# One transformer stack with two kinds of attention and two mixtures of experts: key sums by TensorE, places by the eight largest, one register load per block, weights loaded behind the attention loop

## The chip, the cores and the metric

One core of a Trainium2 chip runs the whole computation. The core has five engines that run their own instruction streams and meet at semaphores: TensorE (PE, matrix products into PSUM), VectorE (DVE), ScalarE (ACT), GpSimd (POOL) and SyncE (SP, which here only issues DMAs). The metric is the time of one execution on the device in microseconds (us), lower is better.

## The reference

`x` is 1024 tokens of 256 channels. Four residual steps follow each other:

```python
x = x + tanh(g_xattn[0]) * L0_xattn(layernorm(x), ctx)   # 16 heads of 16, fake-quantized q, k, v and softmax
x = x + tanh(g_ffn[0])   * L0_ffn(layernorm(x))          # 32 experts of 176 units, 8 chosen in 4 of 8 groups, + shared 352
x = x + tanh(g_xattn[1]) * L1_xattn(layernorm(x), ctx)   # 8 heads per batch over channels, 32 wide
x = x + tanh(g_ffn[1])   * L1_ffn(layernorm(x))          # 32 experts of 96 units, 6 chosen, + shared 192
```

In `L0_ffn` the sigmoid scores plus a bias are taken in 8 groups of 4; a group's score is the sum of its two largest; four groups stay; the eight largest of what is left are the token's experts, and their scores, normalized, are the weights. `L1_ffn` takes the six largest of 32 directly. In `L1_xattn` a head's output is `softmax(q^T k) v^T`: the softmax divides by the sum of the exponentials over the 256 keys.

## The kernel before

Tokens lie in 8 tiles of 128 (NT = 8). Every engine has its own program, written out as loops over numbered steps; the order in each program is the order of execution, and semaphores join them. After the projections (to about 85 us) come these stages.

**Attention of layer 0.** 128 steps s (tile, head). TensorE computes the scores of 1024 keys (`scores`), VectorE their maximum (`row_max`, L1297), ScalarE the exponential (`exp`, L1156), GpSimd the 8-bit form (`quantize`, L1667), SyncE a transposing DMA (`turn`, L745), TensorE the product with v (`attend`, four steps late). Three times per 32 steps, work for the pair of tiles just finished ("unit" u = 0, 1, 2) is slipped in at fixed places `at` of the window: output projection, norm, router, choice of experts (`choose0`, five parts at 22 to 26), place in each expert's list (`place`, two parts at 27 and 29). `place` turns the 0/1 mask of chosen experts into row numbers: a running count over the experts gives each chosen expert a number 1 to 8 (`kq`), `eq` compares it with 1 to 8, `prod` multiplies with the positions from TensorE's `rank`, and a reduction picks them (L1414, L1425, L1426). With these numbers GpSimd scatters the rows of `xaug` (the normed token, its places and weights) to `xs_dram` by indirect DMA, one instruction per tile and place (`scatter`, L1680): 64 in layer 0, 48 in layer 1. From step 61 on one is sent in every second step.

**Experts' weights.** SyncE loads 44 tiles for gate and up of layer 0 in eleven DMAs of 1 MB, each waiting for the one before it (`tiles_in`, L751): two inside the attention loop at steps 70 and 86, nine behind it. Then come `blocks_in` (register loads from `tab`, then each block's rows, L774, and down weights, L780).

**FFN of layer 0, then of layer 1.** The unit list `units` holds the shared expert (8 tiles in 3 parts, layer 1: 2 parts) and then the routed blocks of 128 rows (95, layer 1: 79). `ffn(layer, i)` is the step of each engine; for TensorE it transposes block q + 1 (L956), does gate and up of q (L993), turns the hidden values of q - 1 (L1005) and does down of q - 2 (L1026). The expert of a block is a number in `tab`, read into registers of TensorE for four blocks at once (`experts_of`, L962). VectorE finds where each row goes, for four blocks at once (`goes_to`, L1501 to L1514), GpSimd scatters the results to `y_dram` (`y_scatter`, L1690). Unit 3 of layer 0 is chosen and placed inside the steps of the shared expert: `choose0` at i = 9, `place` at 12 and 14, `tables` at 14 and 18.

**Sums.** `sums_in` brings the k rows of every token back (`y2`, a ring of 3 in W), and `routed_sum` adds them with a reduction over a strided view (L1545); in layer 0 GpSimd adds the halves of tiles 2 to 7 first (`half_sum`, L1698).

**Attention of layer 1.** 16 steps n: `scores1`, `row_max1` (L1561), `exp1` with the sums of the keys beside it (L1227), `inverse_sum1` (L1569), `normalize1` on GpSimd (L1706), `turn1`, `turned1`, and per tile `attend1` (L1080) and `tile_out1` (L1582). The sums of layer 0 are worked in at steps 1, 5 and 9, and the choice and places of layer 1 at step 13 and later; unit 3 is done inside the steps of layer 1's shared expert.

## Time and profile before

| | us |
|---|---|
| median of 3 runs | 984.89 (984.3 to 984.92) |
| the profiled execution | 984.9 |
| its span | 983.2 |

| stage | us from the span's start |
|---|---|
| projections and preparation | 0 to 85 |
| attention of layer 0 | 85 to 317 |
| shared expert, places of unit 3, weights | 317 to 388 |
| 95 routed blocks of layer 0 | 388 to 627 |
| sums and attention of layer 1 | 627 to 750 |
| shared expert, scatters of layer 1 | 736 to 804.5 |
| 79 routed blocks of layer 1 | 812 to 948 |
| sums of layer 1, output | 948 to 983 |

Busy over the span: TensorE 730.5 us, VectorE 584.4, GpSimd 500.0, ScalarE 444.1. How to read it: no engine is busy all the time, and each stage has its own bound. So a change is priced stage by stage: which engine or which transfer ends the waits there.

### The profile page before, as it was taken

What the parts mean: (1) busy time and instruction counts of PE and PEld (TensorE: products, weight loads), DVE (VectorE), ACT (ScalarE), POOL (GpSimd) and SP (SyncE); (2) the same over time, 40 slices, a digit from 0 to 9 for tenths busy, and PEclk for the clock granted to TensorE, in tenths of its full rate; (3) what the DMA queues carried; (4) which work ended last, traced back from release to release, by engine and by line L of the source; (5) the groups of instructions that cost most, each with busy time, mean ns of one, the idle gap of its engine ahead of it and who ended that gap; (6) DMA issues with size and microseconds to landing.
All of it is one profiled execution on the core that took longest, in us unless ns stands there. A gap on an engine that the chain in (4) does not pass through costs nothing.

```text
span 983.2 us, 19955 instructions
## 1 busy us (share of the span) xinstructions
PE 730.5 (74%) x5595; PEld 540.4 (55%) x5595; DVE 584.4 (59%) x1344; ACT 444.1 (45%) x1057; POOL 500.0 (51%) x579
## 2 busy tenths in 40 slices
PE   5638777677776875999999999435587649998940
PEld 4625445445454663777777777323355537777730
DVE  5997878968878372444444444275665615454538
ACT  4536787566674211444444444224462105555630
POOL 4433676588887632333333333235558754555530
PEclk9867778576585897999999999756776879999985
DMA  8905999799998875666666666682006435555546
GB/s 278 340 1 105 182 171 158 131 218 205 194 185 172 255 245 168 199 193 205 189 203 184 203 186 188 223 345 106 1 2 191 165 121 162 187 161 186 172 159 203
DMA packets 221971, 175.49 MB, mean 178 GB/s; under 512 B 146586, under 2 KB 200810, under 8 KB 220842
## 3 DMA queue, kind: packets, MB, share of 16 engines
q1 hardware_dynamic: 207866, 132.52, 53.3%
q0 software_dynamic: 13728, 41.17, 11.6%
q8 instruction: 50, 0.82, 0.4%
q14 instruction: 55, 0.45, 0.1%
q10 hardware_dynamic: 272, 0.52, 0.1%
HBM read 87.92 MB, written 52.69 MB: 143 GB/s over the span
## 4 chain that ended last, share of the span: by engine, by line
POOL 26%; issue 24%; PE 15%; DVE 11%; DMA 9%; ACT 5%; SPq 0%; POOLq 0%; DVEq 0%; ACTq 0%
POOL y_dram L1690 12%; POOL xs_dram L1680 6%; DMA pT<-p 6%; ACT e L1156 5%; DVE acc L1545 4%; POOL p L1667 4%; PE psum L993 4%; PE psum L1026 3%; DVE nmax L1297 2%; POOL W L1706 2%; PE psum L982 1%; PE psum L956 1%; PE psum L860 1%; POOL W L1698 1%; DMA W<-y_dram 1%
## 5 line engine op out<-in xcount | busy, mean ns | idle before, releaser
L1690 POOL DMA_INDIRECT y_dram<-ybuf,idxi x174 | 166.9, 959 | 232.2 <-ACT ybuf L1205 225.3
L1493 DVE COPY hT<-psum 88x256 f32<-88x256 f32 (+2 forms) x214 | 74.3, 347 | 241.4 <-PE psum L1005 241.2
L993 PE MATMUL psum<-W,xTs 128*128 x696 | 195.6, 404 | 10.9 <-issue 6.5
L1156 ACT ACTIVATE e<-psum,nmax 128x1024 f32<-128x1024 f32 x128 | 142.5, 1113 | 75.8 <-POOL p L1667 44.2
L1297 DVE TENSOR_REDUCE nmax<-psum 128x1 f32<-128x1024 f32 x128 | 153.0, 1220 | 35.9 <-PE psum L860 23.6
L1667 POOL TENSOR_SCALAR p<-e 128x1024 f16<-128x1024 f32 x128 | 134.5, 1051 | 74.8 <-ACT e L1156 50.3
L860 PE MATMUL psum<-kstack,qstack 128*128 128x512 bf16 x256 | 108.9, 521 | 46.7 <-ACT e L1156 43.0
L1680 POOL DMA_INDIRECT xs_dram<-xaug,posi x112 | 110.1, 983 | 49.2 <-issue 33.2
L993 PEld LDWEIGHTS psum<-W,xTs 128*128 128x128 f32 x696 | 115.0, 191 | 36.0 <-issue 16.0
L1195 ACT ACTIVATE sg<-psum 128x176 f32<-128x176 f32 (+2 forms) x214 | 60.9, 285 | 149.1 <-PE psum L993 83.5
L1205 ACT ACTIVATE ybuf<-psum,dot 128x256 f32<-128x256 f32 x174 | 82.4, 474 | 101.0 <-PE psum L1026 100.6
L873 PEld LDWEIGHTS psum<-osb_v,pT 128*128 128x128 f16 x1024 | 68.0, 104 | 47.9 <-DMA pT<-p 27.3
L956 PE MATMUL psum<-ident,xs 128*128 128x128 f32 x348 | 67.8, 276 | 25.4 <-DMA xs<-xs_dram 25.4
L873 PE MATMUL psum<-osb_v,pT 128*128 128x16 f16 x1024 | 72.0, 176 | 16.5 <-DMA pT<-p 16.0
L1186 ACT ACTIVATE xTs<-psum 128x256 f32<-128x256 f32 x174 | 65.4, 376 | 31.8 <-PE psum L956 31.8
L1005 PE MATMUL psum<-ident,h 128*88 128x128 f32 (+2 forms) x309 | 71.0, 280 | 10.1 <-DVE h L1485 9.6
L956 PEld LDWEIGHTS psum<-ident,xs 128*128 128x128 f32 x348 | 49.7, 143 | 44.0 <-DMA xs<-xs_dram 26.2
L874 PEld LDWEIGHTS psum<-osb_v,unlift 128*128 128x128 f16 x1024 | 62.8, 104 | 19.6 <-issue 16.0
L874 PE MATMUL psum<-osb_v,unlift 128*128 128x16 f16 x1024 | 68.5, 172 | 0.0
L1482 DVE TENSOR_TENSOR h<-sg,psum 128x176 f32<-128x176 f32 (+1 forms) x174 | 66.5, 382 | 0.0
L1005 PEld LDWEIGHTS psum<-ident,h 128*88 128x88 f32 (+2 forms) x309 | 39.5, 128 | 44.5 <-issue 16.5
L1545 DVE TENSOR_REDUCE acc<-W 128x256 f32<-128x1536 f32 (+2 forms) x16 | 40.6, 2537 | 23.0 <-DMA W<-y_dram 23.0
(238 smaller groups left out, 1221.5 us busy)
## 6 DMA issues: line engine op xcount, KB each, us to landing
xs<-xs_dram SPq DMA_DIRECT2D x174, 160.0 KB, 3.2
W<-in_wffn SPq DMA_DIRECT2D x17, 1024.0 KB, 6.9
xs_dram<-zeros SPq DMA_DIRECT2D x2, 5120.0 KB, 25.5
oT<-in_wffn SPq DMA_DIRECT2D x96, 88.0 KB
osb_v<-in_wffn SPq DMA_DIRECT2D x94, 88.0 KB
W<-y_dram SPq DMA_DIRECT2D x8, 1024.0 KB, 6.5
W<-y_dram SPq DMA_DIRECT2D x8, 768.0 KB, 4.5
W<-in_wffn SPq DMA_DIRECT2D x4, 768.0 KB
```

The source lines that it names most:

```text
L860: last = pe.matmul(bank(s_bank(s) + n), qstack[:, t // TH, head, t % TH * P:(t % TH + 1) * P], kstack[:, head, n * BANK:(n + 1) * BANK], s ...
L873: pe.matmul(out, pT[:, s % PT_RING, k, :], v, start=k == 0, stop=False)
L874: last = pe.matmul(out, unlift[:, :], v, start=False, stop=k == NT - 1)
L956: last = pe.transpose(ps[:, k * P:(k + 1) * P], xs[:, slot, k * P:(k + 1) * P], ident[:, :])
L993: last = pe.matmul(out, xTs[:, n % 2, k, :], Wv[layer][:, k, :, :, bass.DynSlice(of_block[q], 1), :], start=k == 0, stop=k == KD - 1)
L1005: last = pe.transpose(bank(4)[0:rows, c * P:(c + 1) * P], h[:, q % 2, c * rows:(c + 1) * rows], ident[:, :])
L1156: act.activation(e[:, s % 2, :], bank(s_bank(s), 2), ACT.Exp, bias=nmax[:, s % S_RING:s % S_RING + 1], accum_out=esum[:, t, head:head + 1] ...
L1205: act.activation(ybuf[:, b % Y_RING, :], bank(5 + item(q) % 2)[:, 0:D], ACT.Copy, scale=dot[:, b % XS_RING, 1:2]).then_inc(cf["y_sb"], 1)
L1297: dve.tensor_reduce(nmax[:, s % S_RING:s % S_RING + 1], bank(s_bank(s), 2), AX.X, ALU.max, negate=True).then_inc(c2["max"], 1)
L1667: pool.tensor_scalar(p16[:, s % P_RING, :], e[:, s % 2, :], PMAX, LIFT, ALU.mult, ALU.add).then_inc(c2["p16"], 1)
L1680: pool.indirect_dma_start(xs_dram[layer][:, :], bass.IndirectOffsetOnAxis(posi[:, t, k:k + 1], 0), xaug[:, t, :], None).then_inc(scattered ...
L1690: pool.indirect_dma_start(y_dram[layer][:, :], bass.IndirectOffsetOnAxis(idxi[:, slot:slot + 1], 0), ybuf[:, b % Y_RING, :], None).then_in ...
```

## The change

Nine edits in one step:

1. `place` drops `kq`, `eq` and `prod`. The positions are multiplied with the mask, and `max` (the eight largest of each token) gives the row numbers, whose base is one higher. It now has four parts, `choose0` six; in a window they stand at 17 to 24 and 27, 28. The group search of `choose0` takes six sums of pairs and one maximum.
2. The other work of a window moves to earlier steps (projection 9 to 7, router 17 to 13, and so on). In the tail `place` and `tables` move from i = 12, 14, 14, 18 to 9, 10, 11, 12, 16.
3. No weight is loaded inside the attention loop: eleven DMAs stand behind it.
4. TensorE loads one expert per block, `expert_in(q + 1)`, behind `gate_up(q)`.
5. `goes_to` is cut in three parts, done one group of four blocks ahead.
6. `normalize1`, `inverse_sum1` and the key sums of `exp1` go. `attend1` adds eight products with a matrix of ones, which give the key sums of every output element; `tile_out1` divides by them.
7. Sums are made of `tensor_tensor` additions in place; GpSimd makes more of them in layer 0 and the first of every second tile in layer 1. The ring `y2` has 4 places, the last of them in `xs`.
8. SyncE loads `y2` of layer 0 first, the weights of layer 1 and its shared expert behind that.
9. The choice and the places of layer 1 for all four units lie in the attention loop of layer 1, and GpSimd sends no scatter of layer 1 between its other work.

```diff
-XS_RING, Y_RING, Y2_RING, IDX = 8, 4, 3, 4
+XS_RING, Y_RING, Y2_RING, IDX = 8, 4, 4, 4
...
-                    if s in (70, 86):
-                        sp.wait_ge(c2["scores"], STEPS // 2)
-                        tiles_in(0, 16 + (s - 70) // 4, 4, cw["gu0"])
-                        loaded += 1
                 sp.wait_ge(c2["scores"], STEPS)
-                for first in (0, 4, 8, 12, 24, 28, 32, 36, 40):
+                for loaded, first in enumerate((16, 20, 0, 4, 8, 12, 24, 28, 32, 36, 40)):
...
-                    sp.wait_ge(cw["gu0"], 16 * loaded)
+                    if loaded:
+                        sp.wait_ge(cw["gu0"], 16 * loaded)
                     tiles_in(0, first, 4, cw["gu0"])
...
+                def expert_in(q):
+                    layer, _, b, _ = units[q]
+                    if b == 0:
+                        pe.wait_ge(cp["tab"], layer + 1)
+                    _, of_block[q] = nc.values_load_multi_w_load_instructions(
+                        tab[0:1, 1, b:b + 1], engines=(mybir.EngineType.PE,), min_val=0, max_val=EXPERTS - 1)
...
                     if q < end:
                         gate_up(q)
+                    if q + 1 < end and routed(q + 1):
+                        expert_in(q + 1)
...
+                    for k in range(2):
+                        for j in range(PER_TILE):
+                            last = pe.matmul(bank(0)[j * HD1:(j + 1) * HD1, D:2 * D], ones[:, 0:HD1],
                                              a1pT[t % 2][:, j, k, :], start=k == 0, stop=k == 1, skip_group_check=True)
...
-                        step(dve.tensor_tensor(prod_, eq_, over_places(pos[:, :, :]), ALU.mult))
-                        step(dve.tensor_reduce(posf[:, :, 0:k], prod_, AX.X, ALU.add))
-                        dve.tensor_copy(posi[:, here, 0:k], posf[:, :, 0:k]).then_inc(cp["placed"], 1)
+                        step(dve.tensor_tensor(pos[:, :, :], pos[:, :, :], mask[:, here, :], ALU.mult))
+                    else:
+                        pick_first(pos, posf, 2)
+                        dve.tensor_scalar(posi[:, here, 0:k], posf[:, :, 0:k], 1.0, None, ALU.subtract).then_inc(cp["placed"], 1)
...
+                        if b % IDX and b - b % IDX + IDX < BLOCKS[layer]:
+                            goes_to(layer, b - b % IDX + IDX, b % IDX - 1)
...
-                    step(dve.tensor_reduce(acc[:, t % 2, :], y2[:, t % Y2_RING, 0:k * D].rearrange("p (k d) -> p d k", k=k),
-                                           AX.X, ALU.add))
+                        step(dve.tensor_tensor(y[:, 0:n], y[:, 0:n], y[:, n:2 * n], ALU.add))
+                    if layer == 1:
+                        step(dve.tensor_tensor(y[:, D:2 * D], y[:, D:2 * D], y[:, 2 * D:3 * D], ALU.add))
+                    elif not pooled(layer, t):
+                        step(dve.tensor_tensor(y[:, 0:2 * D], y[:, 0:2 * D], y[:, 2 * D:4 * D], ALU.add))
+                    step(dve.tensor_tensor(acc[:, t % 2, :], y[:, 0:D], y[:, D:2 * D], ALU.add))
...
-                    dve.scalar_tensor_tensor(x[:, t, :], bank(0)[:, 0:D], tgate[:, 1:2], x[:, t, :], ALU.mult,
-                                             ALU.add).then_inc(cx["x"], 1)
+                    step(dve.reciprocal(inv1[:, :], bank(0)[:, D:2 * D]))
+                    dve.scalar_tensor_tensor(inv1[:, :], bank(0)[:, 0:D], tgate[:, 1:2], inv1[:, :], ALU.mult,
+                                             ALU.mult).then_inc(cx["out"], 1)
+                    dve.wait_ge(cx["out"], t + 1)
+                    dve.tensor_tensor(x[:, t, :], x[:, t, :], inv1[:, :], ALU.add).then_inc(cx["x"], 1)
...
-                half_sum(2)
-                half_sum(3)
...
+                half_sum(0, 2)
+                half_sum(0, 3)
+                for u in range(1, NT // 2):
+                    if u == NT // 2 - 1:
+                        norm_rstd(pool, step, 0, 0, cn[2]["stats"], cn[2]["rstd"])
+                    norm_rstd(pool, step, 2 * u, u, cn[1]["stats"], cn[1]["rstd"], 1.0 / SCALE1 ** 2)
+                    if u < NT // 2 - 1:
+                        half_sum(0, 2 * u + 2)
+                        half_sum(0, 2 * u + 3)
+                norm_rstd(pool, step, 2, 1, cn[2]["stats"], cn[2]["rstd"])
+                for i in range(NT * TOP[1]):
+                    scatter(1, i)
+                    if i == 5:
+                        norm_rstd(pool, step, 4, 2, cn[2]["stats"], cn[2]["rstd"])
+                    elif i == 15:
+                        norm_rstd(pool, step, 6, 3, cn[2]["stats"], cn[2]["rstd"])
```

## Rows read from the trace of the kernel before

**Rows 1.** Windows: busy us (instructions) of PE, PEld, DVE, ACT, POOL; clock; DMA share, GB/s.

```profile
285.40:316.40 31.00, 22.60 (x324) 14.49 (x321) 28.12 (x59) 18.21 (x33) 24.04 (x23) 0.61 0.96 178
316.40:388.00 71.60, 47.21 (x273) 38.66 (x273) 28.06 (x129) 12.14 (x35) 33.42 (x37) 0.81 0.75 229
388.00:627.00 239.00, 238.54 (x1143) 176.11 (x1141) 110.56 (x312) 101.11 (x284) 89.67 (x94) 1.00 0.61 187
652.30:732.60 80.30, 48.03 (x322) 32.59 (x321) 52.42 (x105) 40.05 (x145) 43.46 (x81) 0.71 0.19 70
812.40:943.80 131.40, 120.12 (x702) 100.84 (x702) 64.96 (x255) 76.68 (x231) 71.56 (x75) 1.00 0.53 168
```

**Rows 2.** Waits of SyncE's queue, 320 to 380 us: total us, times, longest us.

```profile
SPq L751 <- DMA W<-in_wffn: 40.3, 7, 7.8
SPq L787 <- DMA xs_dram<-xaug,posi: 8.8, 1, 8.8
```

**Rows 3.** Chain of waits, 376 to 392 us: start, us, what.

```profile
378.98 0.03 SPq L787
...
382.17 2.21 DMA xs<-xs_dram
...
388.31 2.14 PE psum L993 x4
```

**Rows 4.** The same view at the last scatters of layer 1.

```profile
800.79 0.96 POOL xs_dram L1680
...
802.05 2.50 DMA xs_dram<-xaug,posi
```

**Rows 5.** Timeline of TensorE at two neighbouring blocks of layer 1: start, us.

```profile
854.14 0.81 PE L993 MATMUL psum<-W,xTs 128*128 x4
...
855.56 0.81 PE L993 MATMUL psum<-W,xTs 128*128 x4
```

**Rows 6.** Groups by shape, whole span: busy us, mean ns, idle before.

```profile
L1545 DVE TENSOR_REDUCE acc<-W 128x256 f32<-128x1536 f32 x8 | 21.9, 2731 | 9.5 <-DMA W<-y_dram 9.5
...
L1698 POOL TENSOR_TENSOR W<-W 128x1024 f32<-128x1024 f32 x6 | 13.9, 2342 | 0.0
...
L1545 DVE TENSOR_REDUCE acc<-W 128x256 f32<-128x2048 f32 x2 | 7.2, 3587 | 13.4 <-DMA W<-y_dram 13.4
...
L466 DVE TENSOR_TENSOR tok<-tok,inv 128x2048 f32<-128x2048 f32 x2 | 4.6, 2291 | 0.1
...
L463 DVE RECIPROCAL inv<-step_of 128x128 f32<-128x128 f32 x2 | 1.9, 952 | 0.1
```

**Rows 7.** The same of VectorE, 338 to 357 us (tail).

```profile
L1425 DVE TENSOR_TENSOR prod<-eq,pos 128x512 f32<-128x512 f32 x1 | 0.7, 693 | 0.0
```

**Rows 8.** Timeline of VectorE in the attention loop: start, us.

```profile
311.64 1.52 DVE L1425 TENSOR_TENSOR prod<-eq,pos 128x512 f32<-128x512 f32 x1
```

**Rows 9.** Windows of 32 exponentials each (L1156 alone): ACT busy, clock, DMA.

```profile
192.10:254.98 62.88, 37.82 (x64) 0.66 1.08 210
254.99:317.66 62.67, 37.82 (x64) 0.64 0.99 182
```

**Rows 10.** Chain of waits behind the last block of layer 0.

```profile
627.73 5.90 DMA y_dram<-ybuf,idxi
```

**Rows 11.** VectorE by shape in layer 1's attention, 652.3 to 732.6 us.

```profile
L1545 DVE TENSOR_REDUCE acc<-W 128x256 f32<-128x1024 f32 x6 | 11.6, 1928 | 0.0
...
L1547 DVE TENSOR_TENSOR x<-x,acc 128x256 f32<-128x256 f32 x6 | 2.5, 424 | 0.2
...
L1569 DVE RECIPROCAL a1rs<-a1sum 128x4 f32<-128x4 f32 x14 | 2.4, 169 | 1.1 <-ACT W L1227 1.1
```

**Rows 12.** TensorE's queue at a register load, 850.8 to 852.4 us: ns, first and last start.

```profile
L962 PEldq FUSED_REGOPS  x4: 146/148/151, 851.3 to 852.1; - x4
...
L962 PEldq TENSOR_LOAD <-tab x1: 330/330/330, 850.9 to 850.9; - x1
```

**Rows 13.** The same queue's wait ahead of gate_up, 852.3 to 853.4 us.

```profile
L991 PEldq EVENT_SEMAPHORE  x2: 51/51/51, 852.4 to 853.3; - x2
```

More of the change, by code:

```diff
@@ L140, in build @@
         mout = sb("mout", [P, 2, EXPERTS + 2])
-        pairs = [sb(f"pairs{i}", [P, 2, GROUPS]) for i in range(8)]
+        pairs = sb("pairs", [P, 2, GROUPS, 6])
         gpad = sb("gpad", [P, 2, GROUPS + 8 - GTOP])
@@ L150, in build @@
         kx = sb("kx", [P, 2, EXPERTS])
-        kq = sb("kq", [P, 2, EXPERTS])
         pos = sb("pos", [P, 2, EXPERTS])
@@ L830, in _ @@
                     sums_in(0, t)
-                    if 2 <= t < 6:
-                        tiles_in(1, 4 * t, 4, cw["gu1"])
+                shared_in(1)
+                for first in range(0, TILES[1], 4):
+                    tiles_in(1, first, 4, cw["gu1"])
                 sp.wait_ge(cx["pT_ps"], 2 * PAIRS1)
@@ L1264, in _ @@
                 norm_apply(act, 0, 0, cn[1]["rstd"], cn[1]["xn"])
-                for i in range(2 * NT + 6):
+                for i in range(2 * NT + 8):
+                    u, at = divmod(i - 9, 4)
+                    if at == 0 and 0 <= u < NT // 2:
+                        norm_apply(act, 2 * u, u, cn[2]["rstd"], cn[2]["xn"])
+                    elif at == 1 and 0 <= u < NT // 2:
+                        x_out(1, u)
+                    elif at == 2 and 0 <= u < NT // 2:
+                        route_out(1, u)
                     if i < 2 * NT and i % 4 == 3 and i // 4 < 3:
@@ L1350, in choose0 @@
[L1350 to L1357 removed]
+                        four = sf.rearrange("p t (g i) -> p (t g) i", g=GROUPS)
@@ new lines, in goes_to @@
+                    if part == 0:
+                        step(dve.tensor_tensor(own[:, 0:n, :], expert_no[:, :].unsqueeze(1).to_broadcast([P, n, EXPERTS]),
+                                               block_expert[:, blocks].unsqueeze(2).to_broadcast([P, n, EXPERTS]),
+                                               ALU.is_equal))
+                    elif part == 1:
+                        for i in range(b, b + n):
+                            dve.wait_ge(xs_in[i % XS_RING], 16 * ring_turn(layer, i, XS_RING))
+                        step(dve.tensor_tensor(both[:, 0:n, :, :], xs[:, slots, D:].rearrange("p n (c e) -> p n c e", c=2),
+                                               own[:, 0:n, :].unsqueeze(2).to_broadcast([P, n, 2, EXPERTS]), ALU.mult))
+                    else:
+                        if ring_turn(layer, b, XS_RING) > 1:
+                            dve.wait_ge(cf["y_sb"], done_before(layer, b + n - 1, XS_RING))
+                        step(dve.tensor_reduce(dot[:, slots, :], both[:, 0:n, :, :], AX.X, ALU.add))
+                        step(dve.copy_predicated(idxf[:, blocks], filled[:, blocks], dot[:, slots, 0]))
+                        for i in range(b, b + n):
+                            earlier = ring_turn(layer, i, Y_RING) - 2
+                            if earlier > 0:
+                                dve.wait_ge(y_out[i % Y_RING], 16 * earlier)
+                        dve.tensor_copy(idxi[:, slots], idxf[:, blocks]).then_inc(cf["idx"], n)
@@ L1610, in _ @@
                     elif i == 9:
-                        for part in range(5):
+                        for part in range(6):
                             choose0(part, 3)
+                        place(0, 0, 3)
+                    elif i == 10:
+                        place(1, 0, 3)
+                    elif i == 11:
+                        place(2, 0, 3)
+                        place(3, 0, 3)
                     elif i == 12:
-                        place(0, 0, 3)
-                    elif i == 14:
-                        place(1, 0, 3)
@@ L1718, in _ @@
                         sent += 1
-                while sent < 44:
+                while sent < 42:
                     scatter(0, sent)
```

343 lines of the change are left out of this document (121 added, 222 removed).

## The prediction

> **What bounds the kernel now.** I read the windows first, stage by stage, then the chain of waits inside each, then the groups by shape for the prices. Six stretches matter. In the attention loop of layer 0 the 15 steps that hold the choice and the places take 31.0 us, and VectorE is busy for 28.1 of them [rows 1]: these steps are VectorE's, 2.07 us each, while elsewhere GpSimd and the transposing DMAs set a shorter step. In the tail (316 to 388) no engine is full; its end is a chain of transfers [rows 2, 3]. The 95 blocks of layer 0 are TensorE's alone: 238.5 busy of 239.0 [rows 1]. The attention of layer 1 runs at 80.3 us with VectorE at 52.4 and TensorE at 48.0 at a clock of 0.71, so it lives on waits between engines. From 736 to 804.5 GpSimd issues scatters, one every 1.26 us [rows 4], 48 of them: 60.5 us. The 79 blocks of layer 1 take 131.4 us for 78 distances, 1.685 each [rows 1], though two neighbours without a register load stand 1.42 apart [rows 5]. Behind them come eight sums of 2.73 us [rows 6].
>
> **Attention loop, three windows: -10 us.** Per unit VectorE loses `eq` and `prod` (0.69 each without company) and the reduction (of the same size), `kq` and four small operations (some 0.6 together), and gets two eight-largest, a product and a subtraction (0.5): 2.2 us less (0.69 from [rows 7]). Beside GpSimd `prod` took 1.52 instead of 0.69 [rows 7, 8]: 0.8 us of waiting goes with it. So 3 us per window, three windows, 9. The new parts are below 1 us each, so a step is 1.22 for the maximum plus at most 1; the two long steps go, and nothing new comes late but GpSimd, whose two quantizations and one scatter fill about 3.5 us of two steps. The two loads that leave the loop cost little: the 32 exponentials beside them took 62.9 us, the next 32 took 62.7 [rows 9]. I take 1. Bounds: 3 x 2.2 = 6.6 less 1.6 for worse places of the other work, and 3 x 4 + 2 = 14. I take 10, nearest to the rows.
>
> The Trainium skill (SBUF — State Buffer, section "SBUF: two separate sides") says that a VectorE operation with two SBUF inputs and a GpSimd operation that reads SBUF exclude each other for the whole instruction. The 1.52 against 0.69 agrees. That rule speaks against edit 7, and it is weighed there.
>
> **Tail: +4 us.** The chain of loads begins when the last transpose is issued (320.4). Seven of its waits sum to 40.3, 5.8 each, with 0.4 for the issue [rows 2]. The wait for the scatters ended 8.8 us after the last load was issued, at 378.98 [rows 2, 3], so that load was issued at 370.2 and would land at about 376.5. Two more in the chain: the eleventh is issued near 382.1. SyncE then takes 3.2 us for its registers (378.98 to 382.17), so the first block's rows are asked for at about 385.9 instead of 382.2, behind half a load, and land at 388.5 instead of 384.4; 3.9 us on, the first routed gate_up (388.3 before [rows 3]) begins at 392.2, all relative to the end of the loop: +4. The places of unit 3 come about 4 us earlier (i = 11 for 14, and 2.2 us less work), the scatters are done by about 375, and that is covered: the weights are late now. Bounds: 0 (loads at 5.2 without scatters beside them, rows asked for in their shadow) to +7.
>
> **Blocks of layer 0: 0 us.** TensorE is full; a register load every block runs in its queue while matmuls of 2.49 us drain. If that cover failed, it would cost up to 0.68 x 95 = 65 us; the third rival.
>
> **End of layer 0 to the last scatter of layer 1: -28 us.** (a) The last result row landed after 5.90 us because weights went ahead of it (edit 8); the unloaded value nearest is the 2.50 of a scatter [rows 4, 10]: -3.5. (b) Sums of tiles 0 and 1: 3.59 + 0.42 each now [rows 6, 11]; as additions 128x1024 (half of 2.29, with overhead 1.2), 128x512 (0.69), twice 0.42 and gaps, 2.9: -2.3 for both. So the first maximum of the attention comes at 652.3 - 5.8 = 646.5. (c) From there to the first placement (732.6 before) VectorE was busy 52.4. Edits: six reductions of 1.93 become one addition of 0.42 each, -9.0; the small reciprocals go, -2.4 [rows 11]; choice and place, -1.9; placement one step earlier in the program, two maxima and a copy less, -3.1; and five `tile_out1` gain a reciprocal of 128x256. A reciprocal of 128x128 took 0.952 [rows 6], so 1.8, with 0.4 for one more addition: +2.2 each, +11. That leaves 47. GpSimd's normalizing is gone, but each half sum grows from 2.34 [rows 6] to some 3.5, and VectorE's additions wait for it; TensorE gets as many more matmuls per tile as `attend1` has now. Of the 28 us of waits (80.3 - 52.4) I keep 16: the start (norm, scores), two or three collisions with half sums, and slow-clock matmuls. First placement: 646.5 + 63 = 710. (d) GpSimd has nothing else left then, so 48 scatters run through: 48 x 1.26 = 60.5, two norms of 1.4, landing 2.5: 776 instead of 804.5. Placements of the other units come every 13 to 15 us or faster, ahead of 12 scatters (15.2); the 16 steps of the shared expert begin behind the last placement (about 745) and end before 776 too. Bounds: no waits at all, 696 and -42; all 28 kept, 721 and -17. I take -28.
>
> **Blocks of layer 1: -10 us.** One load of four registers takes TensorE's queue 1.5 us (850.9 to 852.4 [rows 12, 13]; 0.33 for the load, then 0.29 per register), and TensorE stood still for part of it [rows 12]. One register per block is then 0.39 + 0.29 = 0.68. Between two passages of the same wait the queue needed 0.9 us (0.86) for a whole block without a load [rows 13]. 0.86 + 0.68 = 1.54, above TensorE's 1.42 [rows 5]: the queue becomes the bound, at 1.54 per block. 78 x (1.685 - 1.54) = 11.3; some stalls at the block ring stay, 10. The three parts of `goes_to` take away what delayed `down` once in four blocks, inside the same 1.54. Bounds: fully hidden, 1.42 and -20; each load fully open, 1.42 + 0.68 = 2.10 and +32.
>
> The rule that speaks against this edit is in the Trainium skill (DMA: Bandwidth & Descriptors, "Latency and other measured facts"): a register load has a floor of about 600 ns, and the compiler takes four at once to amortize it. The row has 0.33 for the instruction, less than that floor; what the floor would make of the time is rival 5.
>
> **Last sums: -3 us.** A tile costs VectorE 2.73 + 0.42. An even tile becomes 0.95 + three of 0.42, 2.4 with gaps; an odd one 1.76 on GpSimd (3/4 of 2.34 [rows 6]) and 1.35 on VectorE. If the two engines exclude each other, as `prod` shows, a pair costs 2.4 + 1.76 + 1.35 = 5.5 against 6.2: 2.8 for four pairs. If they overlap, 8.
>
> **Sum.** -10 + 4 - 28 - 10 - 3 = -47. The profiled execution took 984.9 (1.7 around its span of 983.2), the median of the runs is 984.89: 938.
>
> **The rivals.** (1) The register loads hide wholly: 1.42 per block, 928. For: in layer 0 the same load costs nothing; against: 0.86 + 0.68 > 1.42. (2) VectorE keeps all its waits in the attention of layer 1, now for half sums and for TensorE's products: -17 in place of -28, 949. For: the reciprocal and the longer half sums stand on the same two engines; against: the normalization that held TensorE is gone. (3) Slower than before: the queue has no room, and every register load is open, 0.68 us in each of 95 blocks (+65) and 2.10 per block in layer 1 (+32 in place of -10): 984.9 - 10 + 4 - 28 - 3 + 97 = 1045. It decides the sign as soon as 0.33 us of every load are open in both layers: 95 x 0.33 = 31 and 78 x (0.33 - 0.265) = 5 are 36, against the 37 gained in the other stages. For: each load of four cost layer 1 up to 1.06 us (4 x (1.685 - 1.42)). Against: 238.5 of 239.0 in layer 0 with 1.5 us loads in it. (4) The loop gains only 4 and the weights cost 7: the loads take what the loop gave, 947. (5) A load that stands alone holds the queue longer than the load in front of a group of four: in a group the three further registers lie in the shadow of the first answer, so the 0.33 of the row is only the part that shows. The whole group is 1.5; if a quarter of the 0.87 of those three was such shadow, a single load holds 0.68 + 0.21 = 0.89, the queue needs 0.86 + 0.89 = 1.75 per block, above 1.685, and layer 1 loses 78 x 0.065 = 5: 984.9 - 10 + 4 - 28 + 5 - 3 = 953. For: no row shows a load alone. Against: each of the four register instructions has a length of its own behind the load, 0.15 [rows 12]. The floor of 600 ns named above would be this case.
>
> **How the numbers follow.** Forecast 0.5, rival 1 0.15, rival 2 0.17, rival 4 0.08, rival 5 0.05, rival 3 0.05. The range 915 to 962 holds the forecast with its bounds (-14 to -5, 0 to +7, -36 to -17, -20 to -3, -8 to 0, not all at once), rivals 1, 2, 4 and 5; outside are rival 3 and the far ends. What this kernel can tell from no change is 0.2%, 2 us. Faster 0.94, same 0.01, slower 0.05.
>
> **What would show it.** Steps 17 to 28 of a window at most 2.2 us apart, and no 1.5 us `prod`. The eleventh load landing after the last scatter of unit 3. Layer 0's blocks still 2.49 apart with TensorE above 99%. The first scatter of layer 1 near 710 less the earlier gain of 6, then 48 in a row. Blocks of layer 1 1.54 apart with even gaps; 1.42 means rival 1. Reciprocals of 1.8 us in `tile_out1`. Wrong would be: blocks of layer 0 longer than 2.49, or scatters waiting for placements of later units.

## The result

The changed kernel takes 951.29 us (median of 4 runs, 948.25 to 955.92) against 984.9 of the kernel before (4 runs, 984.3 to 985.09): a ratio of 0.9664, with an interval of 0.962 to 0.9708. Forecast was 938 with a range of 915 to 962. The profiled execution took 949.4 us with a span of 947.6, so the span is 35.6 shorter; 47 were forecast.

The table cuts both spans at the same instructions: first and last exponential of layer 0, first gate_up, last scatter of results, first maximum of layer 1, first and last scatter of `xaug`, first and last gate_up. The last column is the forecast term. All come from one profile each; how far the changed kernel's profiles differ stands ahead of the experiments.

| stretch | before | after | difference | forecast |
|---|---|---|---|---|
| to the first exponential | 86.5 | 84.9 | -1.6 | 0 |
| attention loop of layer 0 | 229.9 | 220.5 | -9.4 | -10 |
| tail, to the first gate_up | 71.7 | 75.0 | +3.3 | +4 |
| blocks of layer 0, to the last scatter | 239.6 | 243.7 | +4.1 | 0 |
| to the first maximum of layer 1 | 24.6 | 18.7 | -5.9 | -5.8 |
| to the first scatter of layer 1 | 83.5 | 65.0 | -18.5 | -22 for these |
| first to last scatter of layer 1 | 66.2 | 69.9 | +3.7 | two rows |
| to the first gate_up of layer 1 | 10.3 | 10.4 | +0.1 | 0 |
| 78 distances of blocks of layer 1 | 131.4 | 121.8 | -9.6 | -10 |
| to the end | 39.4 | 37.7 | -1.7 | -3 |

Six rows came within 1.3 us of their term, and the 1.6 us of the start are its own spread (84.6 to 86.7 over the profiles of the changed kernel and its variants). Two terms failed: the blocks of layer 0 (+4.1 for 0) and the scatters of layer 1 (the two rows give -14.8 for -22). These two are 11.3 us; the span lies 11.4 above the sum, and what is left cancels.

### The profile page after: what moved, and what is told of

Its sections match the earlier page's. It is cut to its first block, busy times and chain, and to the rows that moved or that the text cites. A ratio compares the mean times of both kernels' runs of the same rounds, so it can differ in the third digit from the quotient of the medians.

```text
span 947.6 us, 20145 instructions
## 1 busy us (share of the span) xinstructions
PE 741.3 (78%) x5723; PEld 545.1 (58%) x5723; DVE 552.8 (58%) x1322; ACT 438.9 (46%) x993; POOL 485.8 (51%) x524
## 4 chain that ended last, share of the span: by engine, by line
PE 37%; DMA 16%; POOL 13%; DVE 9%; issue 8%; ACT 5%; SPq 2%; POOLq 0%; DVEq 0%; ACTq 0%
PE psum L974 13%; PE psum L1007 10%; DMA W<-in_wffn 6%; DMA pT<-p 6%; POOL y_dram L1652 5%; ACT e L1134 4%; POOL xs_dram L1642 4%; POOL p L1629 4%; PE psum L941 3%; PE psum L986 2%; DVE nmax L1268 2%; DMA W<-y_dram 2%; PE psum L845 2%; DVE a1nb L1528 1%; DVE inv L1542 1%
## 5 line engine op out<-in xcount | busy, mean ns | idle before, releaser
L1134 ACT ACTIVATE e<-psum,nmax 128x1024 f32<-128x1024 f32 x128 | 142.5, 1114 | 60.8 <-POOL p L1629 41.8
L1629 POOL TENSOR_SCALAR p<-e 128x1024 f16<-128x1024 f32 x128 | 133.8, 1045 | 66.4 <-ACT e L1134 42.6
L1164 ACT ACTIVATE xTs<-psum 128x256 f32<-128x256 f32 x174 | 65.4, 376 | 34.8 <-PE psum L941 34.8
L941 PEld LDWEIGHTS psum<-ident,xs 128*128 128x128 f32 x348 | 50.0, 144 | 46.8 <-DMA xs<-xs_dram 28.8
L986 PE MATMUL psum<-ident,h 128*88 128x128 f32 (+2 forms) x309 | 69.9, 277 | 7.2 <-DVE h L1439 4.1
L986 PEld LDWEIGHTS psum<-ident,h 128*88 128x88 f32 (+2 forms) x309 | 39.2, 127 | 39.4 <-issue 16.4
L1007 PE MATMUL psum<-W,hT 96*128 x158 | 54.4, 427 | 0.0
```

The costliest lines, as they stand in the source:

```text
L941: last = pe.transpose(ps[:, k * P:(k + 1) * P], xs[:, slot, k * P:(k + 1) * P], ident[:, :])
L986: last = pe.transpose(bank(4)[0:rows, c * P:(c + 1) * P], h[:, q % 2, c * rows:(c + 1) * rows], ident[:, :])
L1007: last = pe.matmul(out, hT[0:rows, q % 2, c * P:(c + 1) * P], w, start=part == 0 and c == 0, stop=ends(q) and c == parts - 1)
L1134: act.activation(e[:, s % 2, :], bank(s_bank(s), 2), ACT.Exp, bias=nmax[:, s % S_RING:s % S_RING + 1], accum_out=esum[:, t, head:head + 1] ...
L1629: pool.tensor_scalar(p16[:, s % P_RING, :], e[:, s % 2, :], PMAX, LIFT, ALU.mult, ALU.add).then_inc(c2["p16"], 1)
```

## The profile after

Windows of the changed kernel, columns as in [rows 1]: end of the attention loop, tail, blocks of layer 0, attention of layer 1 to the first placement, blocks of layer 1.

```profile
284.90:305.40 20.50, 15.65 (x222) 10.10 (x220) 18.51 (x38) 13.07 (x22) 16.82 (x17) 0.58 1.06 180
305.40:380.40 75.00, 48.21 (x289) 39.70 (x290) 25.94 (x122) 12.18 (x36) 34.32 (x38) 0.77 0.84 253
380.40:624.10 243.70, 239.70 (x1143) 176.68 (x1141) 102.11 (x312) 101.20 (x284) 90.87 (x94) 0.99 0.59 182
642.90:706.90 64.00, 51.34 (x386) 33.75 (x385) 54.24 (x95) 33.14 (x80) 25.36 (x31) 0.77 0.40 146
788.20:909.90 121.70, 121.65 (x701) 101.12 (x701) 59.97 (x258) 76.70 (x231) 71.53 (x75) 0.99 0.57 180
```

Against [rows 1], layer 0 holds the same 1143 matmuls in 243.7 us with 239.7 busy: 4 us of standing still, where there was 0.5. TensorE's timeline shows that it is one place, between the gate_ups of blocks 4 and 5. The lines are blocks 3, 4 and 5, counted from 0:

```profile
387.19 1.35 PE L974 MATMUL psum<-W,xTs 128*128 x4
389.68 1.35 PE L974 MATMUL psum<-W,xTs 128*128 x4
395.91 2.38 PE L974 MATMUL psum<-W,xTs 128*128 x4
```

6.23 us in place of 2.49. The chain of waits there names the cause (start, us, what), and the waits of VectorE from 380 to 396 us its size:

```profile
388.82 3.68 DMA xs<-xs_dram
...
392.62 0.44 DVE both L1460
...
393.43 0.45 DVE h L1436
```

```profile
DVE both L1460 <- DMA xs<-xs_dram: 5.5, 1, 5.5
```

L1460 is the second part of `goes_to`, now one group ahead: at block 2 VectorE waits for the rows of blocks 4 to 7, the last of which SyncE asked for at 388.8, and the hidden values (`h`) that TensorE needs stand behind that wait in VectorE's queue.

The scatters of layer 1 do not run through. GpSimd's timeline at its two norms (in brackets the idle time ahead):

```profile
714.35 0.96 POOL L1642 DMA_INDIRECT xs_dram<-xaug,posi  x1 [0.30 <-issue]
720.30 0.23 POOL L268 TENSOR_SCALAR shift<-mv 128x2 f32<-128x2 f32 x1 [4.99 <-DVE mv L262]
...
733.70 0.96 POOL L1642 DMA_INDIRECT xs_dram<-xaug,posi  x1 [0.30 <-issue]
736.62 0.23 POOL L268 TENSOR_SCALAR shift<-mv 128x2 f32<-128x2 f32 x1 [1.96 <-DVE mv L262]
```

The norms of units 2 and 3 stand after scatter 6 and 16, and GpSimd waits 4.99 and 1.96 us for VectorE's statistics with the places of more scatters in hand.

VectorE by shape from 642.9 to 706.9 us (answers to [rows 11]):

```profile
L1542 DVE RECIPROCAL inv<-psum 128x256 f32<-128x256 f32 x5 | 8.7, 1748 | 0.0
L1515 DVE TENSOR_TENSOR acc<-W 128x256 f32<-128x256 f32 x4 | 4.1, 1026 | 0.0
```

The reciprocal costs 1.75 us, close to the 1.8 taken from the 128x128 one. The additions of `acc` have 1.03 on average for 0.42 without company. Four additions of this window, each beside a half sum of GpSimd's, took 1.07 to 2.24 us; together with the other 13 of their shape they are 5.2 us over 0.42 each.

TensorE's queue at one register load in layer 1 (answers to [rows 12]):

```profile
L949 PEldq TENSOR_LOAD <-tab x2: 300/301/302, 850.7 to 852.2; - x2
L949 PEldq FUSED_REGOPS  x1: 151/151/151, 851.1 to 851.1; - x1
L949 PEldq SEQ_ASSERT  x1: 18/18/18, 851.3 to 851.3; - x1
```

One load per 1.5 us, no longer than one in front of a group of four (0.33).

At the end (timeline of VectorE and GpSimd, then the last instructions of GpSimd's and VectorE's queues), an addition of 0.42 takes 1.91 beside GpSimd:

```profile
927.26 2.23 POOL L1662 TENSOR_TENSOR xs<-xs 128x768 f32<-128x768 f32 x1 [1.74 <-DMA xs<-y_dram]
927.88 1.91 DVE L1512 TENSOR_TENSOR W<-W 128x256 f32<-128x256 f32 x1
929.82 0.43 DVE L1515 TENSOR_TENSOR acc<-W 128x256 f32<-128x256 f32 x1
```

```profile
L732 POOLq DRAIN  x1: 8443/8443/8443, 938.9 to 938.9; - x1
L732 DVEq DRAIN  x1: 464/464/464, 941.9 to 941.9; - x1
```

## The experiments

Each was timed in rounds with the kernel before. Times are medians, the ratio is to the kernel before, and stretches are those of the table, from one profile each. Where a stretch is unedited, the profiles differ: the loop has 220.5 to 223.1 us, the tail 74.3 to 79.7 (eight profiles), the blocks of layer 0 241.6 to 245.6 where they have the stall, the 78 distances of layer 1 121.3 to 125.4 (nine), first to last scatter 68.0 to 70.0. The end, 37.3 to 38.2, is steady, and so is the usual distance of two blocks of layer 1, 1.53 to 1.54 at the median. A smaller difference than these spreads shows nothing.

The times need the same care. Ten runs of the changed kernel lie between 948.3 and 957.4 us. Only e8 and e10 lie wholly below them; the medians of e4, e5 and e9 are below the lowest, that of e1 above the highest. For e2, e3, e6 and e7 the time alone shows nothing, and the reading is that of the stretches.

**The changed kernel again (e0).**

> The changed kernel once more, nothing edited, to learn its own spread: its four times lay between 948.3 and 955.9 us, those of the kernel before within 0.8 us. If the spread belongs to the kernel, five more rounds fall in the same 8 us band around 951 and a second profile shows which stage carries it. I expect the variable part in one of two places: the stall at the fourth and fifth block of layer 0 (3.9 us in the first profile), or the eleven weight loads behind the attention loop (65.6 us for eleven). If the spread came from one odd process only, all fall within 1 us of each other.

952.98 us, six runs from 948.4 to 957.4. The spread belongs to the kernel; in these rounds the kernel before spread too (981.8 to 987.7). The stall at blocks 4 and 5 is in every profile with this order, of 2 to 6 us, mostly 4. What varies most over the profiles is the tail, by the weight loads (eleven took 64.9 us where the tail has 74.3, and 69.9 where it has 79.7): the second of the two places named. The blocks of layer 1 vary too, by a wait of the third part of `goes_to`, where VectorE waits for result scatters to land. Its total, number and longest, 788 to 910 us:

```profile
DVE idxi L1471 <- DMA y_dram<-ybuf,idxi: 9.9, 17, 1.4
```

In e5 one scatter took longer (chain of waits), and two neighbouring distances were 3.42 and 2.73:

```profile
847.66 5.64 DMA y_dram<-ybuf,idxi
```

**Loads of four again (e1).**

```diff
-                    _, of_block[q] = nc.values_load_multi_w_load_instructions(
-                        tab[0:1, 1, b:b + 1], ...
+                    if b % IDX == 0:
+                        _, four = nc.values_load_multi_w_load_instructions(tab[0:1, 1, b:b + n], ...
+                        for i, one in enumerate(four):
+                            of_block[q + i] = [one]
```

> Only the number of registers per load is undone: four experts at once in every fourth block, at the same place behind gate_up. Theory (TensorE's queue): the load of four holds the queue 1.55 us, more than the work that lies in front of TensorE covers, so the pattern of 1.42, 1.6, 2.1, 1.5 per four blocks comes back in layer 1, 1.66 on average for 1.54 to 1.56 now: +8 us (+6 to +11), all in the 79 blocks of layer 1; layer 0 stays at 2.49. Rival (the gain came from goes_to in three parts, which no longer delays down): layer 1 stays at 1.54 to 1.56 and the time within 1 us.

960.1 us (0.9746, 0.9715 to 0.9776). The 78 distances took 132.6 us for 121.8: +10.9, at the theory's upper end (+7 against the longest of the nine profiles, and the time is 7 to 9 above the changed kernel's medians). The gate_ups of three blocks:

```profile
850.91 0.82 PE L978 MATMUL psum<-W,xTs 128*128 x4
853.33 0.81 PE L978 MATMUL psum<-W,xTs 128*128 x4
854.75 0.81 PE L978 MATMUL psum<-W,xTs 128*128 x4
```

2.42, then 1.42 three times: about 1.0 of a load's 1.55 us is open and 0.56 hidden, which is 1.42 - 0.86. With one register 0.68 - 0.56 = 0.12 is open: 1.54. The rival fell.

**One register per block in the kernel before (e11),** the same edit from the other side.

```diff
-                    if kind == "routed" and index % IDX == 0:
-                        ...
-                        for i, expert in enumerate(experts_of(layer, index)):
-                            of_block[q + i] = expert
...
                     if q < end:
                         gate_up(q)
+                    if q + 1 < end and routed(q + 1):
+                        expert_in(q + 1)
```

> The kernel before with edit 4 alone: one expert register per block, read behind gate_up of the block before; goes_to stays whole, in every fourth block. Theory (the load is hidden in layer 0 and the queue is the bound in layer 1): no stall at blocks 4 and 5 of layer 0 (that belonged to goes_to one group ahead), 239.6 us from first gate_up to last scatter as before, and in layer 1 1.54 to 1.6 for three of four blocks with a longer fourth where goes_to delays down: 78 distances in 122 to 127 us for 131.4, -5 to -9, about 977 for 985. Rival (goes_to in three parts is half of the gain): 127 to 131 us, -1 to -4. If the stall belonged to the register loads, layer 0 gets 4 us longer.

974.31 us (0.989, 0.9859 to 0.9921). The windows for the blocks of both layers:

```profile
387.90:626.90 239.00, 237.88 (x1143) 175.41 (x1141) 109.78 (x312) 101.15 (x284) 90.08 (x94) 1.00 0.61 188
810.60:932.00 121.40, 121.28 (x702) 100.69 (x701) 65.30 (x257) 76.69 (x231) 71.49 (x75) 1.00 0.57 181
```

121.4 for 131.4: the edit gives 10 us alone (11 in the time), more than expected, and `goes_to` in three parts gives nothing measurable to layer 1. Layer 0 has no stall at blocks 4 and 5, so that one belongs to edit 5.

**No bounds check in TensorE's queue (e9).**

```diff
-                        tab[0:1, 1, b:b + 1], engines=(mybir.EngineType.PE,), min_val=0, max_val=EXPERTS - 1)
+                        tab[0:1, 1, b:b + 1], engines=(mybir.EngineType.PE,), min_val=0, max_val=EXPERTS - 1,
+                        skip_runtime_bounds_check_because="tab's experts are held to 0 to 31 by tables")
```

> The instruction that checks the loaded expert's bounds is left out of TensorE's queue (the values are held to 0 to 31 where tab is written). Theory (in layer 1 the queue is the bound at 1.51 to 1.54 us per block): the instruction stands 0.14 us of it (851.24 to 851.38), so the distance falls to 1.42 to 1.45 and layer 1's 78 distances give back 5 to 8 us; layer 0, TensorE-bound at 2.49, gives nothing. Rival (VectorE and ScalarE, not the queue, set 1.54): no change in layer 1.

947.14 us (0.9618, 0.9594 to 0.9642); 78 distances in 117.5 us for 121.7. In the queue the register operation of 0.15 us went with the check, so that the load alone is left:

```profile
L949 PEldq TENSOR_LOAD <-tab x1: 303/303/303, 849.8 to 849.8; - x1
```

Most distances are now 1.42, TensorE's own (65 of 78 are at most 1.44; 2 with the check); single ones of 1.6 to 3.6 us remain, one load among the 77 took 0.70. So the queue was the bound at 1.54, as the forecast had it. The gain, 4.2, is below the 5 to 8 expected: 0.11 per block would be 8.6, but the waits for result scatters have 14.5 us here for 9.9. As they vary from profile to profile (e8 has 13.2 with the check), the 4.2 says less than the 0.11.

**The second group at block 4 (e2).**

```diff
+                        if b == IDX:
+                            for part in range(3):
+                                goes_to(layer, IDX, part)
-                        if b % IDX and b - b % IDX + IDX < BLOCKS[layer]:
+                        if b > IDX and b % IDX and b - b % IDX + IDX < BLOCKS[layer]:
```

> goes_to for the second group of four blocks is done whole at block 4, not in parts at blocks 1 to 3; all other groups as in the change. Theory: in layer 0 VectorE stood at block 2 in its wait for the rows of block 7, which SyncE had asked for last (landed 392.5 us), with the product of the hidden values queued behind it; distances of 6.23 and 3.52 for 2.49. With the group later the stall goes: -4 us in layer 0's first ten blocks, and at most -1 at the first distance of layer 1 (2.56). Rival: the rows of blocks 4 and 5 are themselves late because SyncE issues 1.55 us of DMAs per block and reads its tables twice: then TensorE waits there instead and 0 to -1 is seen.

949.99 us (0.9649, 0.9616 to 0.9682), and 243.2 us for the blocks of layer 0: nothing gained. Neither theory held as put. The distances of blocks 4 to 6 are 2.49, but those at 7 and 8 are 3.07 and 5.73: the stall moved one group on. What stops VectorE is not the place of one group but that SyncE is not far enough ahead for any of them.

**SyncE's tables early (e5).**

```diff
                     tiles_in(0, first, 4, cw["gu0"])
+                    if loaded in (8, 9):
+                        sp.wait_ge(cp["tab"], 1)
+                        early[IDX * (loaded - 8)] = table_of(0, IDX * (loaded - 8))
```

> SyncE reads the rows and experts of the first eight blocks while the ninth and tenth weight loads are under way (tab was ready at 352), not behind the last one. No DMA is moved but by that. Theory (SyncE's lead sets the stall at blocks 4 and 5, since goes_to one group ahead asks for rows two blocks earlier than before, and SyncE needs 4 x 1.56 + 3.2 = 9.4 us per four blocks against 9.96 of TensorE, so it cannot catch up): SyncE is 3.2 us earlier at block 0 and 6.4 at block 4. First gate_up about 3 us earlier (377.5), of the stall of 3.9 us some 0.7 is left: -5 to -6. Rival (rows land late because the DMA engines are still full of weights): the stall stays at 3 to 4 us and the start moves by 0 to 1.

946.35 us (0.9618, 0.9596 to 0.9641). The stall is gone, all distances from the third on are 2.49, and the blocks take 239.8 us for 243.7. So SyncE's lead was it (e10, with the tables early too, has no stall either): edit 5 asks for rows two blocks sooner, and a SyncE that needs 9.4 us per four blocks of 9.96 cannot make up for that but by a stall. The start did not move (tail 75.2): xs asked for at 372.3 landed 5.8 us later, behind the last weights, and the last 1 MB landed at 377.5.

**Two loads in the loop again (e4).**

```diff
                     turn(s)
+                    if s in (70, 86):
+                        sp.wait_ge(c2["scores"], STEPS // 2)
+                        tiles_in(0, 16 + (s - 70) // 4, 4, cw["gu0"])
```

> Edit 3 alone is undone: two of the eleven weight loads lie at steps 70 and 86 of the attention loop again, nine behind it. Theory (the weights end the tail): in the changed kernel the last load landed at 376.1 us, the last scatter of unit 3 twelve us earlier (issued 360.4, about 363 landed). With nine loads the last lands 5.9 x 2 = 12 us earlier, level with the scatters; the loop gets 1 us longer: first block at about 370 for 380.5, -9 to -11 in all, near 941. Rival (in the loop the DMA engines are full, share 0.96 to 1.08, so 2 MB more delay the transposes by as much as they save behind it): loop 6 to 10 us longer, total within 3 us of the changed kernel.

947.26 us (0.963, 0.9603 to 0.9657). The tail took 68.3 us for 74.3 to 79.7, the loop 224.4 for 220.5 to 223.1. The exponentials of the window that holds both loads, first of the changed kernel, then of this one:

```profile
187.87:247.15 59.28, 37.59 (x64) 0.59 1.03 189
```

```profile
188.26:251.46 63.20, 37.82 (x64) 0.62 1.08 210
```

+3.9 us for two loads where I had put 1 (the same window, 56.9 us from first to last exponential in the changed kernel, has 56.9 to 57.9 in all profiles without loads and 60.8 here: 3 to 4), and -7 behind the loop where 12 were expected (6 to 11 below the eight tails): between theory and rival. The comparison in [rows 9] had misled. Without loads the second window is 1.4 us shorter than the third (56.9 and 58.3, first to last exponential), so two equal windows did not mean free loads; how much VectorE's long steps hid there stays open.

**Two loads in flight (e8).**

```diff
-                    if loaded:
-                        sp.wait_ge(cw["gu0"], 16 * loaded)
-                    tiles_in(0, first, 4, cw["gu0"])
+                    done = cw[("gu0", "gu0b")[loaded % 2]]
+                    if loaded > 1:
+                        sp.wait_ge(done, 16 * (loaded // 2))
+                    tiles_in(0, first, 4, done)
```

> The eleven weight loads behind the attention loop alternate between two semaphores, so that two are under way and not one; nothing else. Theory (the chain is serial and leaves the DMA engines idle between a landing and the next transfer: DMA share 0.84 in the tail, 5.1 us for the shortest, 6.0 on average): eleven take 50 us or less for 65.6, the last lands by 363, and the scatters of unit 3 (issued to 360.4, landed 363) become the end: first routed gate_up 370 to 373 for 380.5, and -4 to -10 for the time, as the stall at blocks 4 and 5 stays. Rival (the DMA engines are full, the scatters pay for the loads): last landing 1 to 3 us earlier, scatters later, total 0 to -2.

945.27 us (0.9585, 0.9565 to 0.9605), five runs within 3.4 us. Eleven loads took 48.6 us (313.3 to 361.9) for 64.9 to 69.9, and the tail 66.8 for 74.3 to 79.7. What the DMA queues moved in 40 slices of the stretch of the loads, in the changed kernel and in this one:

```profile
GB/s 226 211 331 348 341 135 284 388 86 112 394 316 56 357 405 199 191 391 54 101 336 407 208 227 390 421 159 325 314 351 188 247 386 35 241 358 11 202 400 210
```

```profile
GB/s 221 217 207 250 207 356 280 402 427 402 407 407 413 338 388 375 378 333 244 347 295 347 362 414 277 211 350 309 299 362 399 173 287 255 320 384 415 423 393 288
```

With one load at a time the rate falls to 11 to 112 GB/s between loads. The theory held: the chain was serial, not full. (The first gate_up is at 375.2 and not at 370 to 373, since this loop ended 2.9 us later.)

**Norms later (e3).**

```diff
-                    if i == 5:
+                    if i == 11:
                         norm_rstd(pool, step, 4, 2, cn[2]["stats"], cn[2]["rstd"])
-                    elif i == 15:
+                    elif i == 23:
```

> GpSimd makes the norms of units 2 and 3 of layer 1 after scatter 12 and 24, not after 6 and 16. Theory A: the two waits of GpSimd inside the scatters (4.99 and 1.96 us) are a plain loss from the in-order queue; without them the scatters end 7 us earlier, about 944 for a profile of 949.4. Theory B: behind them stands the placement of unit 1, which came at 728.4; 12 scatters from 707.9 end at 723.1, so the same queue then waits 5 us for it, and only the second norm's wait is gained: -2.5 us (-1 to -3.5).

949.48 us (0.9656, 0.9626 to 0.9687). First to last scatter 66.2 us for 69.9, -3.7. GpSimd's next idle time:

```profile
730.30 1.07 POOL L1642 DMA_INDIRECT xs_dram<-xaug,posi  x1 [3.22 <-DVE posi L1381]
```

Behind the order in GpSimd's queue stands the placement of unit 1: theory B. But not all of the 3.7 is the edit. This profile ran at a higher granted clock of TensorE's, and so did that of e5, whose order of norms is the old one. From 30 us behind the first maximum to the first scatter, in the changed kernel, here and in e5:

```profile
672.90:707.90 35.00, 28.82 (x230) 19.52 (x229) 30.96 (x64) 18.50 (x45) 9.09 (x16) 0.81 0.02 7
```

```profile
678.80:710.50 31.70, 25.71 (x232) 16.92 (x229) 30.41 (x64) 18.02 (x44) 8.59 (x16) 0.94 0.01 3
```

```profile
670.30:702.00 31.70, 25.68 (x232) 16.88 (x229) 30.40 (x64) 18.05 (x44) 8.61 (x15) 0.94 0.02 6
```

The two with 0.94 have the first scatter 61.7 us after the first maximum, the others, at 0.81 to 0.87 and without an edit ahead of it, 64.4 to 65.4. That the clock is the cause is likely but not shown (TensorE was busy for 25.7 us in place of 28.8). e5 has 68.0 from first to last scatter, so against it the norms gain 1.8; against the changed kernel, e10 (clock 0.86, the same norms later) gains 2.7. So the order is 1.8 to 2.7 of the 7 us lost.

**Transposes behind the products (e7),** on top of e3: `x_transposed(1, u)` behind `attend1` on TensorE, `x_out` behind `turned1` on ScalarE.

```diff
-                    if at == 0 and 0 <= u < NT // 2:
-                        x_transposed(1, u)
...
                         attend1((i - 4) // 2)
                     if at == 0 and 0 <= u < NT // 2:
+                        x_transposed(1, u)
                         route(1, u)
```

> On top of the norms after scatter 12 and 24: in layer 1's attention the transposes of the normed tokens (x_transposed) stand behind attend1 of the same step in TensorE's order, and ScalarE's copy of them behind its exponentials; before, TensorE waited 1.9 and 3.4 us for ranked with the turns of the attention behind it. Theory (TensorE's order holds the placement of unit 1, which came at 728.4 and for which GpSimd then waits 4.5 us): the placement comes 2 to 4 us earlier and so does the last scatter: 63 to 64 us from first to last scatter for 66.2. Rival (the chain of unit 1 is bound by its own length: transposes, router, choice, rank, places, 20 us): no gain, or a loss of up to 2 because the copy of unit 0 now comes later.

952.2 us (0.9656, 0.9627 to 0.9685). First to last scatter 65.1, 1.1 less than in e3, but the first scatter came 66.4 us after the first maximum (61.7 in e3, 65.0 in the changed kernel). Between last result and last scatter it is 3.4 us slower than e3: the rival. But e3 had the high clock, and this profile has 0.81. Against e10, whose norms stand in the same place at 0.86, it is 0.8 us slower (150.1 for 149.3). How much of this is the edit stays open; a gain is not shown.

**Last sums on VectorE alone (e6).**

```diff
-                    return t >= 2 if layer == 0 else t % 2 == 1
+                    return layer == 0 and t >= 2
-                for t in range(1, NT, 2):
-                    half_sum(1, t)
```

> GpSimd's share in the last sums is left out: all eight tiles are added by VectorE (0.95 + three of 0.42, 2.34 us a tile with gaps). In the changed kernel VectorE's additions of 0.42 us took 1.9 beside GpSimd, and the sums lasted 20.8 us (921.5 to 942.3) plus the output. Theory (the two engines exclude each other, so the share of GpSimd buys nothing): 8 x 2.34 = 18.7, -2 us (-1 to -4, the last also for the tile that waited 1.8 us for GpSimd behind its own load). Rival (GpSimd takes a real part): +2, eight tiles at 2.34 are behind the loads and the overlap is lost.

948.86 us (0.9624, 0.9597 to 0.9652). From the last gate_up to the end 32.3 us for 37.7: -5.4, more than either bound. The sums give 2.7 (18.1 us for 20.8). The other 2.7 lies behind them: GpSimd's drain takes 8.4 to 8.8 us, behind an addition and behind scatters (8.76 in the kernel before, where it is hidden). In the changed kernel it ran from 938.9 to 947.4, 2.9 us past the output's landing at 944.4; here it starts behind the scatters and is hidden:

```profile
L732 POOLq DRAIN  x1: 8660/8660/8660, 918.3 to 918.3; - x1
```

**All together (e10):** two loads in flight, SyncE's first two tables read before its wait for the scatters (both layers), no bounds check, norms later, last sums on VectorE. The edit that no other experiment has:

```diff
+                    early = {b: table_of(layer, b) for b in (0, IDX)}
                     sp.wait_ge(scattered[layer], 16 * NT * TOP[layer])
                     for b in range(BLOCKS[layer]):
                         if b % IDX == 0:
-                            table = table_of(layer, b)
+                            table = early[b] if b in early else table_of(layer, b)
```

> Two loads in flight, the tables of the first eight blocks read before the wait for the scatters (both layers), no bounds check, norms after scatters 12 and 24, the last sums on VectorE alone. From the changed kernel's 951: tail -8, stall at blocks 4 and 5 -4, attention and scatters of layer 1 -3.5, tables of layer 1 -1.5, blocks of layer 1 -6, last sums -2: -25, 926. If the parts collide (the rows of the first blocks behind the last weights, a scatter queue that is not the end any more), 935.

918.61 us (0.9324, 0.9288 to 0.936): 33 us below the changed kernel, 7 more than expected. Tail, blocks of layer 0, blocks of layer 1 and end:

```profile
307.80:371.00 63.20, 48.95 (x290) 40.32 (x291) 25.84 (x122) 12.15 (x35) 34.26 (x38) 0.82 0.91 297
371.00:610.20 239.20, 237.96 (x1142) 175.76 (x1141) 102.40 (x312) 101.14 (x284) 90.26 (x95) 1.00 0.60 186
...
766.40:884.40 118.00, 113.90 (x703) 99.77 (x702) 60.15 (x259) 76.70 (x231) 71.45 (x75) 1.00 0.59 187
884.40:916.60 32.20, 2.82 (x13) 1.61 (x11) 18.29 (x37) 2.14 (x5) 4.30 (x5) 0.60 0.67 249
```

Against the changed kernel's profile: tail -11.8, layer 0 -4.5, attention and scatters of layer 1 -4.3, scatters to first gate_up 6.9 for 10.4 (the tables), blocks of layer 1 -3.8, end -5.4, and +2.4 before the tail.

## Why the prediction was right, and where it was not

**Attention loop.** The sum was right (-9.4 for -10; -6.8 to -9.4 over the unedited profiles), its parts were not. Windows 1 and 3, from first to last exponential, lost 3.9 and 3.1 us; window 2, which held both loads, lost 4.7, and with the loads put back (e4) only 0.8 (61.6, 56.9 and 60.8 us). So the loads cost 3 to 4 where I took 1, and VectorE's part is about 8 where I took 9. One sign was missed: steps 17 to 28 of a window were to be at most 2.2 us apart, and two maxima there stand up to 2.74 apart (before, up to 4.96), with one of 4.3 at step 14 of the last two.

**Tail.** +3.3 for +4, by the step forecast: the last scatter was issued at 360.4, the last load landed at 376.1. That the number is so near is luck: eight profiles give +2.6 to +8.0 over the 71.7 of before. What I did not ask is whether the chain must be serial; e8 shows that it was the chain, not the bandwidth.

**Blocks of layer 0: the first wrong step.** "0 us" looked only at the register load, which is indeed hidden (e11: 239.0). Edit 5 I had priced in layer 1's queue alone. Moving a wait one group ahead is a new wait: it asked for rows two blocks earlier of a SyncE that had no such lead. The prediction should have set SyncE's 9.4 us per four blocks against 9.96. Its own sign of being wrong, distances above 2.49 in layer 0, came true; e5 shows the cause.

**To the last scatter of layer 1: the second.** Its parts (a) to (c) held: 5.9 for 5.8, and 64.0 us from the first maximum to the first placement for 63.5, though with 54.2 us of VectorE's work and 9.8 of waits in place of 47 and 16. The sum is right because the two misses cancel, which is luck; 5.2 of the 7 us more work are additions stretched beside GpSimd's half sums. (The lower bound of 696 for this stretch is an error of adding: 646.5 + 47 is 693.5.) The step that failed is (d), "GpSimd has nothing else left then, so 48 scatters run through". It counted the two norms with 1.4 us each and not what they wait for: 4.99 and 1.96 us, the 7 that are missing. The sign named was scatters that wait for placements; they waited for norms. e3 and e10 show that order alone gives back 1.8 to 2.7 of them. Rival 2 has the time (949), but not the cause: VectorE's waits did shrink.

**Blocks of layer 1.** -9.6 for -10 (-6.0 to -10.1 over the nine profiles with this queue), and the mechanism stands on four kernels: load of four 132.6, single 121.8 (and 121.4 in the kernel before), single without check 117.5. The forecast distance of 1.54 is there at the median, 1.53. Rival 1 (1.42 per block) became true only when the queue got shorter. Rivals 3 and 5 fell with the single load's 0.30 us (median of 77, 0.30 to 0.45); the floor of about 600 ns for a register load in the Trainium skill (DMA: Bandwidth & Descriptors, "Latency and other measured facts") does not show here, and the measurement decides.

**Last sums.** -1.7 for -3, and near only because two misses cancel. The price of exclusion held: 5.2 us per pair of tiles (20.8 / 4) for the 5.5 forecast, so the sums gave 4.2 (25.0 before) where 2.8 was forecast. The rule of the Trainium skill (SBUF — State Buffer, "SBUF: two separate sides") agrees: 1.91 us for an addition of 0.42 beside GpSimd. Missed was GpSimd's drain behind its last work, 2.9 us past the output, which took back 2.7. Without GpSimd the same additions give 7 us in place of 1.7.

## What to carry to other kernels

Work that is moved one group ahead brings its waits along: before giving it a place, compare the lead that it asks for with what the producer's queue gains per block. When a stage looks limited by transfers, look at the rate between them; a chain that waits for each load before the next shows holes, and two in flight closed them here. Ask what GpSimd does last, and what it does beside VectorE in SBUF: its share in the last sums cost more than it took off. Whether its larger share in the sums of layer 0 pays was not tested, though four of VectorE's additions are stretched there. And before a few microseconds of one stretch are put down to an edit, compare the granted clock of that stretch in both profiles.

## What the hardware showed that I had not expected

GpSimd's queue ends with a drain of 8.4 to 8.8 us; VectorE's took 0.46. A register load of TensorE's queue took 0.30 us at the median and up to 0.70; two instructions behind it, of 0.15 and 0.02 us, were worth 0.11 us per block at the median and 4.2 us over 78 blocks. Two loads of 1 MB in flight moved eleven in 48.6 us, one at a time in 65.7, and the scatters beside them lost only 0.6 (last one issued at 363.9 us for 360.4, behind a loop that ended 2.9 later). A 128x256 reciprocal took 1.75 us, four times an addition of that shape. In the two profiles where TensorE's granted clock was 0.94 in the second half of the attention of layer 1, in place of 0.81 in the changed kernel, that attention was 3.3 us shorter with no edit to it.
